# Counting edges in groups of one column, with three count tables, zeros in sixteen blocks and a reordered front

## The reference

```python
deg = max(segment_sum(ones, dst), 1); norm = deg ** -0.5
h = relu(layernorm(x))
hw = norm * (h @ W0)
x = x + relu(segment_sum(hw[src], dst) * norm + bias0)      # graph convolution
h = relu(layernorm(x))
for l in range(2):                                          # graph transformer
    q, k, v = h @ Wq.T + bq, h @ Wk.T, h @ Wv.T             # 8 heads of 64
    scores(e) = q[dst(e)] . k[src(e)]; softmax over the edges into a node
    h = batchnorm(h + attention @ Wo.T + bo)
    h = batchnorm(h + feed_forward(h))
return x + layernorm(h)
```

## Time and profile before

| | us |
|---|---|
| median of 3 runs | 3387.66 (3385.79 to 3404.86) |
| the profiled execution | 3393.12 |
| its span in the trace | 3391.3 |
| front, from the start to the first instruction of attention | 989.5 |
| POOL busy in the span | 2155.7 (64%) |
| PE busy in the span | 2990.1 (88%) |

### The profile page before, as it was taken

How to read it: one execution, slowest core, us unless ns; L and a number is a source line. 1 busy time by engine, 2 the same in 40 slices (tenths; PEclk the granted TensorE clock), 3 DMA queues, 4 the chain that set the end, 5 groups by cost and what they waited for, 6 DMA issues and landing times. The chain is left out here.

```text
span 3391.3 us, 72342 instructions
## 1 busy us (share of the span) xinstructions
PE 2990.1 (88%) x24802; PEld 2279.6 (67%) x24802; DVE 2267.0 (67%) x6951; ACT 1965.5 (58%) x3918; POOL 2155.7 (64%) x1991
## 2 busy tenths in 40 slices
PE   2368999978869999999999989989999999999985
PEld 2124655645537778887787877757777778888874
DVE  8594334332337888888888853227888888888856
ACT  0123444433337788888787821227787788888834
POOL 1687877778617777777777710007777777777734
PEclk9999999988989999999999989999999999999998
DMA  9666666645579888888888831238898988888852
GB/s 372 102 126 157 125 122 130 114 91 92 99 194 171 168 166 170 170 175 175 162 167 174 156 84 25 52 72 177 166 166 166 174 171 171 168 173 173 162 120 61
DMA packets 1297462, 496.76 MB, mean 146 GB/s; under 512 B 1237240, under 2 KB 1262865, under 8 KB 1291408
## 3 DMA queue, kind: packets, MB, share of 16 engines
q1 hardware_dynamic: 1156197, 460.22, 63.7%
q0 software_dynamic: 133120, 0.80, 4.2%
q10 hardware_dynamic: 7788, 31.21, 2.8%
HBM read 153.55 MB, written 80.48 MB: 69 GB/s over the span
## 5 line engine op out<-in xcount | busy, mean ns | idle before, releaser
L1255 POOL TENSOR_TENSOR staged<-prob,staged 125x500 f16<-125x500 f32 x960 | 1071.3, 1122 | 166.0 <-ACT staged L1249 87.0
L1483 DVE CUSTOM_DVE_ANT_0 prob<-s_ps,mask 125x500 f32<-125x500 f32 x1600 | 1042.3, 673 | 179.5 <-PE s_ps L1333 116.2
L1420 ACT ACTIVATE prob<-prob,neg_max 125x1000 f32<-125x1000 f32 (+1 forms) x960 | 954.7, 994 | 58.9 <-DVE scrap L1489 53.8
L1333 PE MATMUL s_ps<-keys,queries 128*128 128x500 f16 x3200 | 945.7, 377 | 43.7 <-DMA queries<-q_tiles 28.0
L529 POOL DMA_INDIRECT counts<-count,cell x320 | 653.3, 2042 | 256.3 <-issue 98.1
L1361 PE MATMUL o_ps<-values,across 125*128 125x128 f16 x7680 | 586.8, 219 | 63.9 <-DMA across<-staged 63.4
L1361 PEld LDWEIGHTS o_ps<-values,across 125*128 125x128 f16 x7680 | 502.7, 97 | 200.8 <-issue 70.1
L1249 POOL CAST staged<-prob 125x500 f16<-125x500 f32 x640 | 385.5, 602 | 334.4 <-ACT prob L1420 201.6
L1496 DVE TENSOR_TENSOR p_lo<-t_ps,p_hi 125x500 f16<-125x500 f32 x640 | 434.4, 679 | 171.6 <-ACT p_hi L1430 167.2
L1430 ACT CAST p_hi<-t_ps 125x500 f16<-125x500 f32 x640 | 364.0, 569 | 146.3 <-PE t_ps L1344 145.0
L1344 PEld LDWEIGHTS t_ps<-identity,prob 125*125 125x125 f32 x2560 | 378.2, 188 | 92.0 <-ACT prob L1420 4.4
(11 more groups left out here) (162 smaller groups left out, 3684.2 us busy)
## 6 DMA issues: line engine op xcount, KB each, us to landing
mask<-bias_rows SPq DMA_DIRECT2D x200, 218.8 KB
counts<-xt ACTq DMA_DIRECT2D x8, 3054.0 KB, 37.2
keys<-counts SPq DMA_DIRECT2D x40, 546.9 KB
bias_rows<-edge_bias SPq DMA_DIRECT2D x20, 1093.8 KB
queries<-q_tiles SPq DMA_DIRECT2D x80, 250.0 KB, 3.9
pair_row<-pair_flat SPq DMA_DIRECT2D x40, 437.5 KB
across<-staged SPq DMA_TRANSPOSE x960, 3.0
q_tiles<-q_both SPq DMA_DIRECT2D x80, 125.0 KB, 3.0
```

What stands on the lines that cost most here:

```text
L1255: engine.tensor_tensor(here[0:P, BPC:2 * BPC, 0:P], prob[u % PROBS][:, k * KC:(k + 1) * KC].rearrange("p (s c) -> p s c", s=BPC), here[0:P ...
L1333: mm = pe.matmul(s_ps[n % SB][:, 0:KC], lhsT=queries_sb[b][:, at:at + 128], rhs=keys[:, h, c * KC:(c + 1) * KC], start=(part == 0), stop=( ...
L1420: act.activation(here, here, ACT.Exp, bias=neg_max[u % 4][:, :], accum_out=sums[u // H % 2][:, u % H, piece:piece + 1]).then_inc(exped, 1)
L1483: dve.tensor_tensor_reduce(out=prob[u % PROBS][:, at], in0=s_ps[n % SB][0:P, 0:KC], in1=bias[b][:, at], scale=1.0, scalar=MASKED, op0=ALU. ...
```

## The change

1. `GC` 2 to 1: 320 groups of one column; a column is compared with its own 125 edges. `SIDES` 2 to 3: three tables of their own in DRAM, groups in turn. Before column q POOL waits for column q-3.
2. `load_parts` loads 3 parts of a tile instead of 2 (1.875 MB for 1.25 MB); `merge` has 10 additions for 5, two chained for each piece.
3. Zeros: 16 blocks, each of three DMAs of 781 KB, one for each table (37.5 MB in all for 25.0 MB). ACT writes block 0; SP writes block k behind `load_pairs(k+1)`, after all blocks before have landed. POOL waits only for the blocks that its cells reach, in the first four blocks of tallies (32 columns; DVE works the number out), and for all 16 before column 32.
4. Three buffers for the pair rows, moved to `xt`, like w0.
5. ACT loads x, in two parts, right behind zero block 0.
6. DVE: tallies 0 to 2 stand between the one-hots, tallies 3 behind the statistics of x. `needed` is found from the least destination of each column, by PE and DVE, amid later tallies.
7. The w0 products are pipelined: PE turns tile t+1 ahead of the product of tile t, ACT likewise.
8. `merge(0)` stands ahead of the wait for hw. SP issues `load_parts(0)` before `first_done`, and the ring's x and the weights behind it.

```diff
-GC = 2
+GC = 1
-PER_ROW = 4
+PER_ROW = 8
-SIDES = 2
-ROW = SIDES * N
+SIDES = 3
+SPARE = GE
-ZCOLS = 12216
+ZCOLS = 3052
-ZDMAS = 8
+ZDMAS = 16
+GATED = 4
+ROWS = 3
...
+        def zero_block(engine, k):
+            for n in range(SIDES):
+                engine.dma_start(counts[n][k * ZCELLS:(k + 1) * ZCELLS, :].rearrange("(p r c) o -> p r (c o)", p=128, r=ZREP),
+                                 zero_rows).then_inc(zeroed, 16)
...
-                for k in range(NB):
-                    if k >= 2:
-                        sp.wait_ge(rows_used, k - 1)
+                def load_pairs(k):
+                    if k >= ROWS:
+                        sp.wait_ge(rows_used, k - ROWS + 1)
...
+                load_pairs(0)
+                load_pairs(1)
+                for k in range(1, ZDMAS):
+                    load_pairs(k + 1)
+                    sp.wait_ge(zeroed, SIDES * 16 * k)
+                    zero_block(sp, k)
...
+                for k in range(ZDMAS + 1, NB):
+                    load_pairs(k)
...
-                pool.wait_ge(zeroed, 16 * ZDMAS)
                 for q in range(NG):
                     n, turn = q % SIDES, q // SIDES
                     if q % PER_ROW == 0:
-                        pool.wait_ge(cells_ready, q // PER_ROW + 1)
+                        k = q // PER_ROW
+                        pool.wait_ge(cells_ready, k + 1)
+                        if k < GATED:
+                            blocks = pool.value_load(zeros_due_i[0:1, k:k + 1], min_val=SIDES * 16, max_val=SIDES * 16 * ZDMAS)
+                            pool.wait_ge(zeroed, blocks)
+                            apart(pool, waits_met)
+                        elif k == GATED:
+                            pool.wait_ge(zeroed, SIDES * 16 * ZDMAS)
                     if turn > 0:
                         pool.wait_ge(group_writes[n], 16 * GC * turn)
                         pool.sem_inc(groups_landed, 1)
...
+                onehots(0)
+                onehots(1)
+                tallies(0)
+                for q in range(2, 5):
+                    onehots(q)
+                tallies(1)
+                for q in range(5, QP):
+                    onehots(q)
+                tallies(2)
...
-                    for k in range(NKC):
-                        dve.tensor_tensor(cnt[b][:, piece(k)], parts[b][:, piece(k)], parts[b][:, N + k * KC:N + (k + 1) * KC],
-                                          ALU.add).then_inc(merged, 1)
+                    for k in range(NKC + 1):
+                        if k < NKC:
+                            steps.done(dve.tensor_tensor(cnt[b][:, piece(k)], parts[b][0][:, piece(k)], parts[b][1][:, piece(k)],
+                                                         ALU.add))
+                        if k > 0:
+                            steps.wait(but=1 if k < NKC else 0)
+                            dve.tensor_tensor(cnt[b][:, piece(k - 1)], cnt[b][:, piece(k - 1)], parts[b][2][:, piece(k - 1)],
+                                              ALU.add).then_inc(merged, 1)
...
+                    if t + 1 < NT:
+                        turn_h(t + 1)
+                    times_w0(t)
```

More of the change, by code:

```diff
@@ L151, in sb @@
         return ctx.enter_context(nc.sbuf_tensor(name, shape, dt))
-    counts = dram("counts", [TABLE, 1], U16)
+    counts = [dram(f"counts{n}", [TABLE, 1], U16) for n in range(SIDES)]
     bias_rows = dram("bias_rows", [N, N], F32)
@@ L196, in front @@
     QC = NCOL // QP
[L197 to L202, removed]
+    LC = -(-NCOL // 128)
+    NEEDED = LC * 128
+    XPARTS = 2
+    XT = NT // XPARTS
+    LEAST_AT, NEEDED_AT = 3, 14
+    NORM_AT, LAST_AT = 10, 26
+    counts_rows = [c[SPARE:SPARE + N * N, :].rearrange("(n m) o -> n (m o)", m=N) for c in counts]
+    xt_flat = xt[:, :, :].rearrange("p c n -> p (c n)")
+    zeros = xt_flat[:, 0:ZCOLS // ZREP // 2]
+    w0_sb = xt_flat[:, ZCOLS // ZREP // 2:ZCOLS // ZREP // 2 + FC * D].rearrange("p (c d) -> p c d", c=FC)
     with ExitStack() as ctx:
-        parts = [keys[0:P, 2 * b:2 * b + 2, :].rearrange("p h n -> p (h n)").bitcast(U16)[:, 0:ROW] for b in range(2)]
+        parts = [[keys[0:P, 2 * b + n, :].bitcast(U16) for n in range(2)] for b in range(2)]
+        for b in range(2):
+            parts[b].append(sb(ctx, f"last_part{b}", [P, N], U16)[:, :])
         cnt = [values[:, 2 * b:2 * b + 2, :, :].rearrange("p h t e -> p (h t e)").bitcast(F32)[:, 0:N] for b in range(2)]
@@ L430, in load_parts @@
                         sp.wait_ge(merged, NKC * (t - 1))
-                    for side in range(SIDES):
-                        at = slice(side * N, (side + 1) * N)
-                        load_rows(sp, parts[t % 2][:, at], counts_rows[t * P:(t + 1) * P, at], parts_loaded[t % 2])
+                    for n in range(SIDES):
+                        load_rows(sp, parts[t % 2][n], counts_rows[n][t * P:(t + 1) * P, :], parts_loaded[t % 2])
                 def room_for_x(t):
@@ L547, in tallies @@
                         steps.done(dve.scalar_tensor_tensor(
-                            matches[c % 2][:, :], pair_row[k % 2][:, own], pair[:, at:at + 1],
-                            earlier[:, after:after + GE], ALU.is_equal, ALU.mult, accum_out=tally[:, at:at + 1]))
+                            matches[c % 2][:, :], pair_row[k % ROWS][:, own], pair[:, at:at + 1],
+                            earlier[:, after:after + GE], ALU.is_equal, ALU.mult, accum_out=here[:, c:c + 1]))
                     steps.wait()
@@ L589, in _ @@
-                for k in range(EARLY):
-                    tallies(k)
-                for half in range(HALVES):
-                    for t in range(TH):
-                        steps.done(dve.scalar_tensor_tensor(below[:, t, :], dst_i[:, :], float(P * (half * TH + t + 1)),
-                                                            group_i[:, :], ALU.is_lt, ALU.mult))
-                    steps.wait()
-                    steps.done(dve.tensor_reduce(needed[:, half * TH:(half + 1) * TH], below[:, :, :], AXX, ALU.max))
-                    steps.wait()
@@ L599, in _ @@
-                dve.sem_inc(needed_ready, 1)
-                for k in range(EARLY, AHEAD):
-                    tallies(k)
-                dve.wait_ge(x_loaded, BOTH)
+                dve.sem_inc(needed_ready, 1)
+                onehots(0)
[7 more added lines that the diff above has]
+                tallies(2)
+                dve.wait_ge(onehots_used, QP)
```

255 lines of the change are left out of this document (164 added, 91 removed).

## The result

The median of three runs after is 3498.48 us (3495.24 to 3500.45) for 3387.66 before: ratio 1.032 (95% interval 1.030 to 1.035), slower. The forecast was 3409, its range ended at 3448. The profiled execution has a span of 3498.6 us, 107.3 more than before. Attention's first POOL instruction starts at 1096.75 us instead of 989.54, 107.2 later, so all of the loss lies in the front.

What follows compares the result with a forecast made beforehand. The prediction took the front as bound by POOL's scatter stream to tile 16, then a 197 us serial end. Terms -8 + 15 + 12 - 1 + 3 = +21 us gave 3414 profiled, 3409 as median; range 3365 to 3448.

Steps and rivals of the forecast that it cites:

- rivals 1 and 2: Zero chain slow at 10.4 us a block, 3438 us, chance 0.13; every column caught, waits double, 3451 us, chance 0.13.
- The start: Before column 32: zeros all landed at 160 us, so that column leaves then instead of at 168.75, -8 us (-16 to +21).
- The gate of block 5: Zero block 5 waits until DVE is through with tallies 3; it was to be issued at 75.7 us.
- 5.7 + 1.3 + 0.7 = 7.7 us: One chained zero block: transfer at 409 GB/s, a small store's round trip, half the pair rows; bounds 7.0 and 10.4 us.
- lie mostly in that gap: The 0.5 MB of pair rows (1.2 us) fall mostly in the round trip between zero blocks; half was counted.
- The pace: POOL's scatters: waits on landings +15, parts traffic and costlier regime +12, groups of one -1 us.
- I take a third: POOL's waits on landings to tile 16 grow by between 0 and 49 us; +15 was taken.
- rival 2: POOL's wait before scatters: every column is caught, waits double, 3451 us, decided when waits pass 80 us; chance 0.13.
- Only what falls on a column that is waiting counts: Parts grow 1.5 us a tile over 16 tiles, 0 to 24 us delaying landings; 8 was taken.
- The additions: Merges in the serial end: first piece ready one addition later, 0.7 us on four tiles, +3 us (0 to 13).
- below 3 us: DVE's operations beside POOL's scatters: fewer tallies and doubled merges each stay below 3 us and cancel.
- Rival 5: Tile stage, not stream, sets the front's end; 38 us earlier start would count, 3350 us; chance 0.13 shared with another rival.

## Why the prediction was wrong

The frame held: the front is the start of the stream, its pace, and a serial end, and the tile stage's earlier start is worth nothing. But the start, the waits and traffic of the pace, and the additions were all put too low. What came is rivals 1 and 2 together, which had been priced one at a time. In the prediction's own terms both give 21 + 49 + 20 - 1 + 3 = +92 us, 3480; 3498 came, so even they fall short.

**The start: -8 forecast, +31 measured.** This is the step that failed worst, twice over. The gate of block 5 came 8.8 us late: DVE was 9.1 us behind from its first op (14.84 for 5.79), since the edge list landed late. Zero block 0 and x, issued by ACT at 1.70 and 4.46 us, came beside it (before, the zeros followed at 4.08, x at 28.47). The prediction had taken "the one-hots and what precedes them are as before". And "5.7 + 1.3 + 0.7 = 7.7 us" a block was 10.5. Its upper bound of 10.4 was what came, taken from parts that land amid other traffic; I chose the rate and the round trip of quiet stretches. The sentence that the pair rows "lie mostly in that gap" is refuted by the view of one block: with the end of the zeros they make a phase of their own, 3.6 us at 190 GB/s. The unchained kernels divide it, though the division hangs on the order: with two tables and no chain column 32 leaves at 168.0, as before; three tables in groups of one bring it to 191.9 (+24), the chain to 199.9 (+8). With the chain put on first it is +13 and then +19, and with long rows and paced x the third table costs only 11. In the first of these kernels the 32 early columns gained nothing: x, pair rows and the early scatters share the engines with the zeros, which then take as long as zeros and columns one after the other had.

The page the prediction weighed, the Trainium skill (DMA: Bandwidth & Descriptors, Measured), pointed the right way, for a reason that explains little of it. Its small-DMA figure gave an estimated 8.9 us a block; the trace has 10.5. Small DMAs with short rows do cost, 377 GB/s for 409. But while the zeros have the engines nearly to themselves, the block's view shows 380 GB/s and not 341, and most of what is beyond 7.7 us lies in the last phase.

**The pace: 15 + 12 - 1 = +26 forecast, +59 measured to column 272 and +7 behind it.** "I take a third" was the choice for the waits, and all of the growth came: the waits on landings to column 272 went from 56.5 to 120.4, far beyond the 80 at which rival 2 was to decide. Its parts are not additive. Taken alone the column-wise wait costs 6 us in the kernel before. With two loads in after's order it costs 19 (641.2 for 622.3), with three loads nothing (662.1 for 662.0); both pairs also differ by the third table that the scatters write. The third load costs 40 us under group-wise waits and 21 under column-wise ones. "Only what falls on a column that is waiting counts" underrated it: at three columns' distance nearly every load of parts catches a column. The prediction's own 1.5 us a tile, wholly counted, was 24; the runs have 21 and 40 for 16 tiles, so the larger is not explained by the bytes at 409 GB/s, even if each byte of it counts. With the wait five or six columns back the same loads left 15 us of waits. The distance is the one change of design in which that kernel differs both from the kernel after and from the one with groups of two, two tables and a third load. So it is what turns a late landing into a stall, unless group size and number of tables do it only together: no run changed the distance alone. Why load and column-wise wait don't add is left open.

**The additions: +3 forecast, "0 to 13, if the whole merge counts".** The end behind the stream grew by 9.7 us. Taken alone the additions cost more: 14.2 us in the kernel before and 15.8 in after, so the whole merge counts and a little beyond, some 3 to 4 us for each of four or five serial tiles. Some 6 us came back elsewhere in that end (73.19 before, 67.10 with three loads and two added); the runs don't say where. That PE starts on the first piece 0.7 us later does not help, since what the chain needs next of DVE and ACT stands behind the last piece in their programs. That reason was read from the order of the program; no run tried another order.

They may have a second price, which the prediction had set at "below 3 us": in after one scatter in each of eight tiles takes 2.7 to 3.6 us, and it lies beside a merge. Timeline after, DVE's additions and a scatter:

```profile
757.28 0.68 DVE L756 TENSOR_TENSOR values<-values,last_part 125x500 f32<-125x500 f32 x1
...
757.87 0.68 DVE L752 TENSOR_TENSOR values<-keys 125x500 f32<-125x500 uint16 x1
758.02 3.56 POOL L568 DMA_INDIRECT counts<-count,keys  x1 [6.23 <-DMA counts<-count,keys]
```

This one took 3.56 us for 1.98. Over columns 32 to 272 POOL is busy 496.6 us, and 487.4 where the third part is loaded and not added: 9 us, which the eight slow scatters make up, and half of the additions' 18.7 in the pace. The Trainium skill (SBUF — State Buffer, Who interferes with whom) has it that a DVE instruction with two inputs in SBUF contends with a GpSimd instruction that reads SBUF. In this trace the slow scatters do lie beside such additions. But the kernel with groups of two and three tables has the same additions, and scatters in the midst of them keep their time; none of its 240 takes over 2.5 us:

```profile
611.92 0.67 DVE L752 TENSOR_TENSOR values<-keys 125x500 f32<-125x500 uint16 x1
612.39 2.06 POOL L568 DMA_INDIRECT counts<-count,keys  x1 [0.30 <-issue]
612.51 0.67 DVE L756 TENSOR_TENSOR values<-values,last_part 125x500 f32<-125x500 f32 x1
```

And the kernel before with more additions has two such slow scatters, and POOL busy for only 1.5 us more. So additions alone don't slow a scatter. What makes the eight slow, and the other half of the 18.7 us, stays open.

**The parts that were right, and one that was luck.** The serial chain from tile 16 on, and SP's waits on the stream, though they begin at tile 8 and not at 10 or 11. `merge(0)` came at 277.2 instead of 240: the prediction's 69 us of tallies behind the zeros, counted from 200, and 8 for the parts. POOL's wait before column 32 was 54.9 us where 50 to 70 were forecast, but this is luck: the 32 columns were done at 145 us and not "before about 100", the zeros at 200 and not 160, and the two errors cancel. Rival 5, that the tile stage sets the end, is false of this kernel and true of the one with groups of two and three tables. That one also shows what the stalls were hiding: with them gone the front is as long as before, for PE's pace and the longer serial end then bind. Two streams of nearly equal length stand side by side here, and no version that was run beats the kernel before by more than 0.15% (the one with long zero rows and paced x).

## What to carry to other kernels

Price a transfer by the rate and round trip of a stretch with the same mix of traffic, and count bytes against the engines before looking at who waits: a chain that is taken away frees little when the engines are full. How the bytes are cut and what runs beside them counts as well: the same 37.5 MB were done at 200 us in one form and at 168 in another. For a ring of writes in flight, the distance back to the write that is waited for decided, as far as these runs tell, whether other traffic stalled it; more frequent waits at a short distance are no finer control but more chances to be caught. When several costs are bounded from both sides and all share one resource, their upper ends can come together, as here, and the range has to hold that sum too.

## What the runs showed of the hardware

DMA engines at full share moved 409 GB/s with the long zero rows, 377 with rows and DMAs a quarter of the size, and at shares of 0.92 to 1.07 only 237 to 304 once x, pair rows and scatters ran beside the zeros: the share alone says nothing of bytes. A scatter, for all its smallness, can land very late behind bulk loads. Timeline of POOL in the kernel with long zero rows, two tables, x in two parts:

```profile
61.54 2.82 POOL L574 DMA_INDIRECT counts<-count,keys  x1 [15.90 <-DMA counts<-count,keys]
...
112.48 2.08 POOL L574 DMA_INDIRECT counts<-count,keys  x1 [18.10 <-DMA counts<-count,keys]
```

Waits of 15.9 and 18.1 us for one landing, where the kernel before had 12.2 at most in the earlier trace rows. With x in ten paced parts column 32 leaves 5 us sooner.
